# Head of a fused attention and expert kernel on eight cores: order of the first loads, and a V projection cut in two halves with a lag

## The reference, cut to what matters

```
xn = layernorm(x)                                   # x: [8, 2048, 1024]
# attention, linear in the sequence:
q, k, v = split(xn @ w_qkv.T + b_qkv)
kv  = einsum('bhnd,bhne->bhde', softmax(k, over n), v)
out = layernorm(einsum(silu(q), kv)) * ln_g + ln_b
out = (out * sigmoid((xn @ w_g1.T + b_g1) @ w_g2.T + b_g2)) @ w_out.T + b_out
# experts:
logits = xn @ Wr.T ; top 2 of 8 ; w = softmax(top_vals)
ffn = sum over the 2 of w * (xn @ We[expert])       # each expert takes a bounded number of rows
y = x + out + ffn
```

## Time and profile before

| what | us |
| --- | --- |
| median of 3 runs | 647.52 (644.43 to 647.86) |
| the profiled execution's own time | 645.1 |
| its span on core 7, the slowest | 643.5 |
| spans of the eight cores | 630.1 to 643.5 |

### The profile page before, as it was taken

One profiled execution on the slowest core, in us unless ns is written; L12 is line 12 of the kernel. 1 busy time (PEld: TensorE's weight loads), 2 busy tenths in 40 slices (PEclk: granted clock), 3 DMA queues, 4 the chain that ended last, 5 costly groups with the idle time before them and its releaser, 6 DMA issues.

```text
span 643.5 us, 9261 instructions; the slowest of 8 cores (630.1 to 643.5 us)
## 1 busy us (share of the span) xinstructions
PE 498.5 (77%) x3136; PEld 253.0 (39%) x3136; DVE 267.0 (41%) x609; ACT 220.4 (34%) x339; POOL 158.4 (25%) x148
## 2 busy tenths in 40 slices
PE   0279989967665776999785469895977788989996
PEld 0145555533332334444342224442443344434442
DVE  0537664465754444146656661101111111125555
ACT  0324444342332332355454433442443444310000
POOL 3214435100081000010001142341432220035551
PEclk9979999989886877999997558899999989999999
DMA  9825982999950003600005235899999997237877
GB/s 160 197 78 170 199 231 52 192 223 214 223 101 1 1 0 48 118 0 1 2 0 87 45 99 127 221 245 199 197 218 193 197 273 213 83 113 234 260 219 254
DMA packets 40054, 91.54 MB, mean 142 GB/s; under 512 B 5632, under 2 KB 7808, under 8 KB 40000
## 3 DMA queue, kind: packets, MB, share of 16 engines
q0 software_dynamic: 21024, 44.39, 39.5%
q1 hardware_dynamic: 16528, 38.04, 18.0%
q10 hardware_dynamic: 2448, 8.42, 3.3%
HBM read 87.77 MB, written 28.57 MB: 181 GB/s over the span
## 4 chain that ended last, share of the span: by engine, by line
PE 48%; DMA 16%; DVE 14%; issue 10%; ACT 6%; another core or an unknown queue 2%; DVEq 1%; POOL 1%; ACTq 0%; POOLq 0%; PEldq 0%; SPq 0%
PE PS L298 43%; DMA stage<-xn_d,tabs 9%; DMA wr<-wv_t 5%; PE PS L302 5%; DVE bst L788 2%; ACT stage L306 2%; DMA wlate<-x_tm 2%; DVE nm L683 2%; DVE kacc L326 1%; ACT e_sb L313 1%; DVE stage L322 1%; ACT vq L306 1%; DVE vq L317 1%; DVE nb L322 1%
## 5 line engine op out<-in xcount | busy, mean ns | idle before, releaser
L298 PE MATMUL PS<-wr,xnt 128*128 128x512 bf16 x512 | 118.9, 386 | 13.5 <-DMA wr<-wv_t 5.1
L298 PE MATMUL PS<-xnt,wr 128*128 128x512 bf16 x512 | 128.4, 400 | 0.8 <-ACT vq L306 0.8
L321 DVE TENSOR_SCALAR stage<-PS,wslot_f 128x512 bf16<-128x512 f32 x36 | 26.9, 750 | 155.3 <-PE PS L298 99.1
L302 PE MATMUL PS<-ident_sb,stage 128*128 128x128 bf16 x576 | 43.7, 226 | 47.5 <-DVE stage L314 25.2
L298 PEld LDWEIGHTS PS<-wr,xnt 128*128 128x128 bf16 x512 | 49.3, 99 | 74.6 <-issue 20.0
L298 PE MATMUL PS<-wr,stage 128*128 128x512 bf16 x288 | 68.2, 393 | 7.2 <-ACT stage L313 6.7
L298 PEld LDWEIGHTS PS<-xnt,wr 128*128 128x128 bf16 x512 | 50.1, 102 | 55.9 <-issue 12.4
L298 PE MATMUL PS<-wlate,stage 128*128 128x512 bf16 x288 | 69.5, 397 | 0.8 <-ACTq L112 0.4
L302 PEld LDWEIGHTS PS<-ident_sb,stage 128*128 128x128 bf16 x576 | 38.1, 101 | 62.4 <-issue 52.9
L874 POOL DMA_INDIRECT stage<-xn_d,tabs x40 | 39.1, 979 | 89.2 <-PE PS L302 73.5
L306 ACT ACTIVATE stage<-PS,wslot_f 128x512 bf16<-128x512 f32 x36 | 24.8, 689 | 82.8 <-PE PS L298 69.0
(11 more groups left out here) (138 smaller groups left out, 546.9 us busy)
## 6 DMA issues: line engine op xcount, KB each, us to landing
wlate<-x_tm SPq DMA_DIRECT2D x20, 512.0 KB, 6.3
eo_d<-stage SPq DMA_DIRECT2D x37, 256.0 KB, 32.7
eo_d<-stage SPq DMA_DIRECT2D x8, 768.0 KB, 36.7
wr<-we POOLq DMA_DIRECT2D x3, 2048.0 KB, 17.3
xn_d<-stage SPq DMA_DIRECT2D x16, 256.0 KB, 6.3
wlate<-we POOLq DMA_DIRECT2D x2, 2048.0 KB
vq<-x_tm SPq DMA_DIRECT2D x8, 512.0 KB
wlate<-we POOLq DMA_DIRECT2D x8, 512.0 KB
```

Source lines behind the costliest of these rows:

```text
L298: return PE.run(lambda e: e.matmul(out, l, r, start=start, stop=stop), *toks, sig=sig)
L302: return PE.run(lambda e: e.transpose(out, in_, ident[:]), *toks, sig=sig)
L321: return lane.run(lambda e: e.tensor_scalar(out, a, s1, None, op0=op0), *toks)
```

## The change

1. The DMA of `ltri` is no longer issued at the start but in step 2, after the third normalization (t == 3), and its first user waits for it by a token of its own.
2. The cast copy of the router's weights by DMA is gone. VectorE rounds `wr_f` itself (`head_small`), and all its small preparations now stand behind the first two tiles' statistics.
3. ScalarE takes a square root of a constant first, so that its table is loaded at the start.
4. Tile 2 of x is issued when V's first half has landed (before: when tile 0 had), and tile 3 when tile 2 has landed (before: when tile 1 had). SyncE's list is in order, so everything behind these two waits for them too.
5. Tile 0 is normalized ahead of tile 1's statistics.
6. The second half of V for a tile is computed three steps after the first (s-4 instead of s-1), and the loop has two more steps.

```diff
             x_tok = {0: load_x(0), 1: load_x(1)}
-            x_tok[2] = load_x(2, x_tok[0])
-            x_tok[3] = load_x(3, x_tok[1])
...
             t_idn = GP.move(counter("c_idn"), ident[:], ident_d)
-            GP.move(c_smal2, ltri[:], ltri_d)
             tk = {}
-            t_sm2 = GP.move(c_smal2, wr_hl[:, :, 0:E], wr_t.rearrange("p (c e) -> p c e", e=E))
+
+            act(warm[:], eps_sb[:], AF.Sqrt, t_const)
...
             t_wv = [w_half(0, wv_t, 0), w_half(0, wv_t, 1)]
+            x_tok[2] = load_x(2, t_wv[0])
+            x_tok[3] = load_x(3, x_tok[2])
...
                 if t == 3:
+                    late["ltri"] = GP.move(c_smal2, ltri[:], ltri_d, stat[t])
...
-            t_wrlo = tt(DV, wr_hl[:, :, E:2 * E], wr_f[:], wr_hl[:, :, 0:E], ALU.subtract,
-                        t_wrf, t_sm2)
-            tcopy(DV, io_f[:], io_i[:], t_iota)
...
+            def head_small():
+                a = tcopy(DV, wr_hl[:, :, 0:E], wr_f[:], t_wrf)
+                b = tt(DV, wr_hl[:, :, E:2 * E], wr_f[:], wr_hl[:, :, 0:E], ALU.subtract, a)
+                tcopy(DV, io_f[:], io_i[:], t_iota)
...
             h_stats(0)
             h_root(0)
+            h_norm(0)
             h_stats(1)
-            h_norm(0)
             h_root(1)
-            for s in range(NT + 2):
+            t_wrlo, t_iof = head_small()
+            for s in range(NT + 4):
...
-                v = [h_v(s - 1, h) for h in range(2)] if 1 <= s <= NT else None
+                v0 = h_v(s - 1, 0) if 1 <= s <= NT else None
+                v1 = h_v(s - 4, 1) if s >= 4 else None
...
-                if v:
-                    h_vout(s - 1, 1, *v[1])
+                if v1:
+                    h_vout(s - 4, 1, *v1)
+                if 1 <= s <= NT:
                     trl[s - 1], evl[s - 1] = h_trans(s - 1, lo[(s - 1) % 2], 2, xloT[(s - 1) % 2],
                                                      lo_tok[s - 1], rt.get(s - 3))
-                if s >= 2:
+                if 2 <= s < NT + 2:
                     h_router(s - 2)
```

More of the change, by code:

```diff
@@ L226, in build_nc @@
         half_sb = sb("half_sb", [128, 1], F32)
+        warm = sb("warm", [128, 1], F32)
         bst = sb("bst", [128, 2, 2, 6], F32)
@@ L394, in build_nc @@
             c_wg = counter("c_wg")
-            t_wrlo = tt(DV, wr_hl[:, :, E:2 * E], wr_f[:], wr_hl[:, :, 0:E], ALU.subtract,
-                        t_wrf, t_sm2)
-            tcopy(DV, io_f[:], io_i[:], t_iota)
[L398 to L403, removed]
+            def head_small():
+                a = tcopy(DV, wr_hl[:, :, 0:E], wr_f[:], t_wrf)
+                b = tt(DV, wr_hl[:, :, E:2 * E], wr_f[:], wr_hl[:, :, 0:E], ALU.subtract, a)
+                tcopy(DV, io_f[:], io_i[:], t_iota)
+                tcopy(DV, i_row[:], i_ii[:])
+                tcopy(DV, i_col[:], i_ii[:, 0:NJE])
+                tcopy(DV, vals[:, 1, :], i_tt[:])
+                DV.run(lambda e: e.tensor_scalar(vals[:, 0, :], pz_i[:, 0:1].broadcast_to(
+                    [128, 2 * NT]), float(NSLOT), None, op0=ALU.subtract))
+                return b, tcopy(DV, pz_f[:], pz_i[:])
             stat = {}
@@ L498, in build_nc @@
                                              xnT[:, :, 128 * s:128 * (s + 1)], hi_tok[s], None)
-                if v:
-                    h_vout(s - 1, 0, *v[0])
+                if v0:
+                    h_vout(s - 1, 0, *v0)
                 if s + 2 < NT:
                     h_root(s + 2)
-                if v:
-                    h_vout(s - 1, 1, *v[1])
+                if v1:
+                    h_vout(s - 4, 1, *v1)
+                if 1 <= s <= NT:
                     trl[s - 1], evl[s - 1] = h_trans(s - 1, lo[(s - 1) % 2], 2, xloT[(s - 1) % 2],
                                                      lo_tok[s - 1], rt.get(s - 3))
-                if s >= 2:
+                if 2 <= s < NT + 2:
                     h_router(s - 2)
@@ L550, in r_count @@
             def r_count():
-                mm(bank[7][:, 0:128], ltri[:], hb[:], True, False, tk["hb"], btok[7], t_const)
+                mm(bank[7][:, 0:128], ltri[:], hb[:], True, False, tk["hb"], btok[7], t_const, late["ltri"])
                 for s in range(1, NT):
```

## The result

The changed kernel takes **640.28 us** in the median of 4 runs (638.27 to 662.24), beside 647.29 us for the kernel before (4 runs, 644.43 to 647.86). The ratio is 0.989, with a 95% interval of 0.9847 to 0.9933: faster by about 1.1%. The profiled execution took 640.21 us.

A forecast was written before the change was run, and what follows sets the result against it. The head was taken as a start waiting for DMA, then TensorE-bound. On core 0, 15.0 + 13 + 10.7 = 38.7, plus 72.0 to K, gained 6.2 us; 6.5 on core 7 gave 638.6, plus 2.4: 641.0 us, range 636 to 647.

The forecast's parts named there:

- The forecast case: Whole kernel: K begins 4 to 10 us earlier and later stages follow, 641.0 us; chance 0.60.
- L, V's first half: Head, core 0: time when the first half of V's weights lands, put at 15.0 us, bounds 14 and 17.5.
- Tile 2 and tile 3: Head, core 0: loads of these x tiles, one after the other, 6.5 us each, bounds 10 and 14.4 together.
- V's second half: Head, core 0: second half of V's weights lands at about 26.4 us, 12 us ahead of its use.
- Tile 3 to S: Core 0: from tile 3's landing to S, the start of step 4, first with both V halves: 10.7 us, S at 38.7.
- From S to K: Core 0: TensorE's work from the start of step 4 to K's first matmul, 72.0 us.
- Profiled execution: Whole kernel: 645.1 less a gain of 6.5 on core 7 gives 638.6 us; the median lies 2.4 above.
- V's halves keep their own pace: Rival, V's loads: slow DMA engines need 9.8 us per half whatever else runs; first half at 17.5, time 643.8; chance 0.14.
- Lower clock in steps 1 to 3: Rival, head: TensorE stays at its lower clock between short bursts, costing about 2.5 us, time 643.5; chance 0.06.
- The gain is given back: Rival, after the head: the earlier K start does not reach the end, time 646 to 648; chance 0.11.
- Tile 2 comes too late: Rival, head: V's first half lands no earlier, so x's tiles 2 and 3 are simply later, 649.5 us; chance 0.09.
- At no cost: Head: VectorE's small work, tile 0 normalized first, the early table, ltri's issue and the two added steps cost nothing extra.

The follow-up runs named there:

- e1: Changed kernel, but with x's tiles 2 and 3 released by tiles 0 and 1 as before; 632.75 us, ratio 0.9815.
- e2: Changed kernel with the two small copies issued again ahead of V, into tiles nothing reads; 643.24 us, ratio 0.9974.
- e8: Kernel before with only x's tiles 2 and 3 released later, as in the changed kernel; 645.65 us, ratio 0.993.
- e4: Changed kernel with tiles 2 and 3 both released by V's first half, and V's second half by tile 3; 635.76 us, ratio 0.9849.
- e5: e1 with V's second half issued only when its first half has landed; 632.75 us, ratio 0.976.
- e6: e1 with 16 matmuls of constants, result unread, between the first transposes and V of tile 0; 635.2 us, ratio 0.9773.
- e11: The kernel of e6 run once more; 634.06 us, ratio 0.9832.
- e3: Kernel before with only V's second half computed three steps later and two more loop steps; 635.96 us, ratio 0.9859.
- e9: e1 with the two small copies issued again ahead of V into unread tiles; 644.34 us over 4 runs, 637.64 for the two in the table.
- e12: e1 with x's tile 4 and what stands behind it on SyncE held until V's first half has landed; 632.38 us, ratio 0.9787.

## Why the prediction was right, and where its steps were not

The forecast case came true: 641.0 us against 640.28, K earlier by several microseconds, no wait for V's second half, and the end following K. That the two times lie 0.7 us apart is partly luck. The profiled execution was put at 638.6 and took 640.21; the forecast then added 2.4 us, by which the median before lay above its profiled execution, and this time the median lay 0.1 above. The account of the head was right in order and off in size, with errors that cancel:

- **L, V's first half.** Forecast 15.0 on core 0, measured 15.97 (14.5 to 16.1 over the cores). What the x tiles took from it was put at 3.4 us and is 5.3 (e1, core 0). The start was put at ident's landing, 7.7; ident landed at 9.07, and the half 6.9 us behind it, where the forecast had 7.3 with its tail. Without the small copies the half lands 5.5 us earlier (e2, core 0). The two do not add up: together they brought the half only 7.2 us forward. Behind the small copies, as in the kernel that the 3.4 was read from, x's tiles cost just that much in the mean of the cores (25.2 us before, 21.8 in e8).
- **Tile 2 and tile 3.** Forecast 6.5 each, measured 7.7 and 5.3, sum 13.0 against 13.0. On four other cores tile 3 took 3.5 to 3.9. Tile 2 lands within 0.4 us of V's second half on all cores; without that half beside it, it takes 3.3 to 5.5 (e4).
- **V's second half.** Forecast 26.4, measured 23.9, and 12 us or more ahead of its use in both.
- **Tile 3 to S.** Forecast 10.7, measured 11.5. S is 40.60, not 38.7.
- **From S to K.** Forecast 72.0, measured 71.3. K is at 111.91, not 110.7: a gain of 5.0 on core 0, not 6.2. On core 7 it is 9.5 instead of 6.5, because S is at 38.83, 1.8 us earlier than on core 0, where I had put it 1.5 us later.
- **Profiled execution.** Forecast 638.6, measured 640.21: K on core 7 gained 3.0 us more than forecast, and the end kept 4.9 of those 9.5 us. These two errors cancel as well.

**The rivals.** "V's halves keep their own pace" fell: L is 14.5 to 16.1, not 17.5. The half's landing depends on the other queue's traffic (e1), not on what is queued behind it (e5). "Lower clock in steps 1 to 3": only the first 8 V matmuls took 3.57 us, the next two bursts 1.89 and 1.67 (7 matmuls in the record); by e6 and e11 the slow start is worth 1.7 us of K. "The gain is given back": K's start moved 7.5 us in the mean of the cores and the ends of the spans 4.9. Over the kernels of the table, from K's first matmul to the end takes 516.4 to 520.2 us (517.4 before, 520.0 in the changed kernel) with no clear order that goes with K's start. A loss after the head that grows with the gain is not shown; e6 and e11, the same kernel, already differ by 1.8 us in that stretch. Where the 2.6 us of this one execution went stays open. "Tile 2 comes too late": even e8, the gates alone, with the small copies still in front of V, begins K 3.6 us earlier than before.

**What the prediction did not see.** It priced the change as a whole and never each part against the others. The parts, as K's start in the mean of the cores:

| step | K's first matmul | |
|---|---|---|
| before | 118.5 | |
| V's second half three steps later (e3) | 109.7 | -8.8 |
| VectorE's and ScalarE's early order (e9) | 111.7 | +2.0 |
| small copies out of V's queue (e1) | 105.3 | -6.4 |
| tiles 2 and 3 behind V's first half (changed) | 111.0 | +5.7 |

The sum is -7.5. Each part is priced in this order only, and in another it can have another sign: on top of the kernel before, the gates gained 3.6 us (e8), and on top of e1 they cost 5.7. "At no cost" for VectorE's early order held in the changed kernel, where tile 2 comes later than anything it could hold up, and not in e9, where it let tile 4 out early. And the 11.40 us for which VectorE idles on tile 2, which the prediction named, were the price of the gates: the prediction asked only whether S would still be earlier than before, not whether it would be earlier without them. The best kernels are e1, e5 and e12, at 631.9 to 632.8 us in the table, beside 640.2 for the changed kernel. By the ratios, each to its own runs of before, it is 0.976 to 0.9815 against 0.989, some 5 to 8 us; e12's interval lies clear of the changed kernel's, those of e1 and e5 overlap it a little.

## What to carry to other kernels

When a change has several parts that cure one wait, price each part on top of the others: here the second cure (the gates) had nothing left to cure and cost 5.7 us of K's start. Before holding back one load for another, see whether anything that stands ahead in an engine's program needs the held one: look for the instruction that will wait for it (statistics of tile 2) and for what is queued behind (the copy that feeds V of tile 0). And look at a queue's bytes a packet before clearing the way for it: 1 KB packets alone ran at 158 GB/s, together with 3.2 KB packets at 234. And when an experiment means to switch something on, see on every core whether it did: in e6 core 0 alone would have said that the warm matmuls did nothing.

## What the runs showed of the hardware

- Two small copies, 32 KB and 16 KB, ahead of a 1 MB load on the software queue delayed its landing by 5.5 us on core 0 and 6.6 in the mean of the cores, 1.4 of it by its later issue (e2). With them there were 1317 packets under 512 B from 5.5 to 9 us on core 0, without them 181; the 16 KB one, which also turns f32 into bf16, took 11.8 us to land.
- A second 1 MB load queued behind the first on that queue does not slow the first (landing at 20.0 to 21.3 us in e1, 20.1 to 21.8 without it in e5).
- Where the software queue (1.0 KB packets) and SyncE's queue both had work, they moved 355 and 324 packets (e1, core 0, 12 to 18 us).
- The issue of x's tile 4 took SyncE 0.33 us in e3, at 20.5 us, and 1.68 us in e9, at 11.5 us (core 2).
- The first 8 V matmuls of the head take 3.4 to 3.6 us and the next 8 take 1.89 (446 and 236 ns each; e1, all cores). Behind 16 matmuls of constants, they took 1.89 on twelve of the sixteen cores of e6 and e11. The idle time between the two does not sort the cores by itself: 1.89 us came behind 1.26 to 3.88 us of idling, and the slower ones behind 2.42 (3.48 us), 2.92 (3.57), 4.00 (2.94) and 5.04 (3.57). The granted clock from 20 to 24 us does: 1.00 on the twelve, 0.50 to 0.68 on the four. Windows of e6, core 0 and then core 7 (us; busy PE, PEld, DVE, ACT, POOL; granted clock; DMA share; GB/s):

```profile
20.00:24.00 4.00, 3.60 (x14) 1.48 (x15) 0.21 (x1) 1.28 (x2) 0.66 (x1) 0.57 1.10 215
```
```profile
20.00:24.00 4.00, 2.78 (x24) 1.69 (x24) 0.62 (x4) 2.02 (x3) 0.77 (x1) 1.00 1.08 216
```

On core 0 the granted clock was 0.57 in the mean, so for most of that time at the 1.2 GHz level, and on core 7 it was 1.00, 2.4 GHz. In e1, and in the changed kernel, the same 3.4 to 3.6 us stand in a stretch whose record says 1.00 (changed kernel, the window of PE alone, core 0: us, busy PE, granted clock, DMA share, GB/s), and why the matmuls were slow there is left open.

```profile
26.00:30.00 4.00, 3.45 (x9) 1.00 0.93 254
```
